# Projections of three attentions: biases added as PSUM is read, tables awaited apart, V taken by VectorE

## What is computed

```python
qkv = jnp.einsum('bsi,oi->bso', x, w_qkv) + b_qkv      # layer 0, self
q = _rope(q, cos, sin); k = _rope(k, cos, sin)         # r_even = even*cos - odd*sin; r_odd = even*sin + odd*cos
qh = _split_heads(q @ wq_w.T + wq_b)                   # layer 0, cross; kh, vh alike on ctx
return (x @ W.T + b).reshape(B, S, H, hd)              # layer 1, self: Q, K and V
```

## Time and profile before

| | |
|---|---|
| median of 3 runs | 9370.65 us |
| the profiled execution, its own time | 9320.69 us |
| its span | 9318.9 us |
| `l0ap_`: SyncE's first load to the last V copy | 28.2 to 206.1 us |
| `l0xp_`: the same | 934.7 to 1042.3 us |
| `l1ap_`: the same | 4400.5 to 4516.4 us |
| mean granted TensorE clock | 0.758 |

### The profile page before, as it was taken

How to read it: one execution, slowest core, us unless ns; L and a number is a source line. 1 busy time by engine, 2 the same in 40 slices (tenths; PEclk the granted TensorE clock), 3 DMA queues, 4 the chain that set the end, 5 groups by cost and what they waited for, 6 DMA issues and landing times. The chain is left out here.

```text
span 9318.9 us, 164285 instructions
## 1 busy us (share of the span) xinstructions
PE 6964.9 (75%) x31345; PEld 2804.8 (30%) x31468; DVE 6784.5 (73%) x47597; ACT 4490.9 (48%) x8515; POOL 3923.4 (42%) x2595
## 2 busy tenths in 40 slices
PE   6998667666666656999666666666656899999983
PEld 2333222222222224555222222222223322222212
DVE  2764599999999993554699999999997344344423
ACT  1564466666666652111476776677655322222220
POOL 0000255454545541221365656556553055555550
PEclk7998666666666665999666776766767999999986
DMA  2000000000000000000000000000000411111113
GB/s 62 26 21 5 34 5 8 5 8 5 8 6 7 8 1 16 14 20 10 35 5 8 5 8 5 8 5 8 5 5 9 161 30 29 29 40 32 29 30 73
DMA packets 81598, 193.31 MB, mean 21 GB/s; under 512 B 23728, under 2 KB 38062, under 8 KB 77230
## 3 DMA queue, kind: packets, MB, share of 16 engines
q1 hardware_dynamic: 72366, 169.98, 6.5%
q10 hardware_dynamic: 8192, 12.59, 0.5%
HBM read 118.97 MB, written 62.76 MB: 20 GB/s over the span
## 5 line engine op out<-in xcount | busy, mean ns | idle before, releaser
L2057 DVE TENSOR_REDUCE l1xc_part_max<-l1xc_by_query 128x1 f32<-128x512 f32 (+1 forms) x1024 | 558.0, 571 | 865.3 <-PE l1xc_by_query L1916 772.7
L557 PE MATMUL l1ac_by_query<-l1ac_k_stack,l1ac_q_stack 97*128 (+1 forms) x1024 | 441.5, 497 | 790.8 <-ACT keep_xT L652 436.3
L2015 ACT ACTIVATE l1xc_prob<-l1xc_less_max 128x512 f32<-128x512 f32 (+1 forms) x832 | 451.3, 594 | 1118.7 <-PE l1xc_less_max L1930 973.7
L745 DVE MAX8 l1ac_cand<-l1ac_score 128x8 f32<-128x32 f32 x8192 | 956.3, 185 | 27.9 <-ACT l1ac_score L652 16.9
L745 DVE MAX8 l1ac_cand<-keep_xT 128x8 f32<-128x32 f32 x8192 | 953.4, 183 | 4.4
L557 PE MATMUL l0xc_by_query<-l0xc_k_stack,l0xc_q_stack 97*128 (+2 forms) x1024 | 387.9, 448 | 724.2 <-ACT keep_xT L652 505.4
L745 DVE MAX8 l0xc_cand<-l0xc_score 128x8 f32<-128x25 f32 (+1 forms) x8192 | 896.0, 177 | 33.6 <-ACT l0xc_score L652 15.8
L745 DVE MAX8 l0xc_cand<-keep_xT 128x8 f32<-128x25 f32 (+1 forms) x8192 | 897.4, 177 | 4.4
L527 POOL TENSOR_SCALAR l1ac_lost<-l1ac_score,l1ac_tops 128x2048 bf16<-128x2048 f32 x128 | 695.8, 5436 | 472.8 <-DVE l1ac_tops L764 472.8
L1878 POOL TENSOR_TENSOR l1xc_total<-l1xc_total,l1xc_prob 128x2048 f32<-128x2048 f32 (+1 forms) x176 | 793.8, 4510 | 71.5 <-POOL l1xc_v_tile L1888 71.2
L527 POOL TENSOR_SCALAR l1ac_lost<-keep_xT,l1ac_tops 128x2048 bf16<-128x2048 f32 x128 | 696.1, 5438 | 271.6 <-DVE l1ac_tops L764 271.6
(11 more groups left out here) (455 smaller groups left out, 14631.2 us busy)
## 6 DMA issues: line engine op xcount, KB each, us to landing
l1xc_k<-wide_k SPq DMA_DIRECT2D x32, 400.2 KB, 5.2
moe_w<-in_L_ffn_mlp_w_dram SPq DMA_DIRECT2D x16, 512.0 KB, 4.2
wide_q<-l1xp_full SPq DMA_DIRECT2D x8, 1024.0 KB, 3.9
wide_q_parts<-l1xp_parts SPq DMA_DIRECT2D x16, 512.0 KB, 5.3
l1xc_q_hm<-wide_q_parts SPq DMA_DIRECT2D x32, 256.0 KB, 3.8
l1xc_q<-wide_q SPq DMA_DIRECT2D x32, 256.0 KB, 5.7
wide_sums<-l1xc_o_out ACTq DMA_DIRECT2D x64, 128.0 KB, 2.3
l1xf_num<-wide_sums SPq DMA_DIRECT2D x16, 512.0 KB, 11.7
```

The lines of the kernel that those rows point to most:

```text
L557: nc.tensor.matmul(sA[c % 2][:, 0:w], Qm[0:SHIFT_ROW, bass.ds(at + i * P, P)], Kb[0:SHIFT_ROW, bass.ds(at + a, w)], start=True, stop=True) ...
L745: seg = nc.vector.max(new[:, j:8 * NSEG:NSEG], score[i % 4][:, a:a + w])
L2015: nc.scalar.activation(prob[0:n, buf(j), c], yP[c % 2][0:n], ACT.Exp).then_inc(y_taken, 1)
L2057: nc.vector.tensor_reduce(part_max[:, i % 2, c:c + 1], a_bank(i, c)[:, 0:w], AX.X, ALU.max).then_inc(a_taken, 1)
```

## The change

Four things change in `project`.

1. No bias product is left in the loops of Q, K and V. A bias as a column (one value for each output feature) is made once: products of 128 columns by a single one (new L228) turn each row of 128 bias values into a column of the new PSUM bank `cols_bank`, and ScalarE copies them into `bias_cols`. With rotation VectorE adds the column and multiplies by the table in one instruction (new L316, L319), and the factor 0.25 of Q moves into the copies of the weights. Without it ScalarE adds the column in the copy out of PSUM (new L285, `Identity` with a bias operand where there was `Copy`).
2. The bias of V, which lies along the columns of a tile, is spread over 128 rows once by a product (new L221) into `v_bias`, and added as V is read.
3. Weights and biases have a semaphore of their own; TensorE waits for these six loads only. VectorE waits for the tables, and the mask has a third semaphore.
4. VectorE, not ScalarE, takes the tiles of V (new L303): two between the two subtractions of the last unit, the others behind the second. The mask row comes after them.

```diff
-            pe.wait_ge(loaded, n_loads * 16)
+            pe.wait_ge(loaded, 6 * 16)
...
+            nc.tensor.matmul(vbanks[0][:, 0:D], G.ones[0:1, 0:P], bias[:, 2, :], start=True, stop=True)
+            if rope:
+                pe.wait_ge(w_ready, 2 * W_STEPS)
+            for r in range(per):
+                for w in range(2):
+                    for oc in range(KC):
+                        row = (bias, biasR)[r] if rope else bias
+                        mm = nc.tensor.matmul(cols_bank[:, (r * 2 + w) * KC + oc:(r * 2 + w) * KC + oc + 1],
+                                              row[:, w, oc * P:(oc + 1) * P], G.ones[0:1, 0:1], start=True, stop=True)
+            mm.then_inc(cols_formed, 1)
...
-                    mm = nc.tensor.matmul(bank[:, 0:m], bt[:, w, oc * P:(oc + 1) * P], G.ones[0:1, 0:m],
-                                          start=False, stop=True)
                 mm.then_inc(formed, 1)
+            pe.wait_ge(cols_taken, 3)
             for t, (a, m) in enumerate(kt):
...
-                nc.tensor.matmul(vbanks[t % 2][0:m, 0:D], G.ones[0:1, 0:m], bias[:, 2, :],
-                                 start=False, stop=True).then_inc(v_formed, 1)
...
+            act.wait_ge(cols_formed, 1)
+            for w in range(2):
+                at = cols_bank[:, 0:4 * KC].rearrange("p (r w c) -> p r w c", r=2, w=2)
+                nc.scalar.activation(bias_cols[:, 0:per, w], at[:, 0:per, w], ACT.Copy, scale=SCALE[w]).then_inc(cols_taken, 1)
+            act.wait_ge(cols_taken, 2)
+            nc.scalar.activation(v_bias[:], vbanks[0][:, 0:D], ACT.Copy).then_inc(cols_taken, 1)
...
-                        nc.scalar.activation(full[:, u % 2, a:a + m], banks[at % 4][:, 0:m], ACT.Copy,
-                                             scale=0.25 if w == 0 else 1.0).then_inc(taken, 1)
+                        nc.scalar.activation(full[:, u % 2, a:a + m], banks[at % 4][:, 0:m], ACT.Identity,
+                                             scale=SCALE[w], bias=bias_cols[:, 0, w, oc:oc + 1]).then_inc(taken, 1)
...
-            for t, (a, m) in enumerate(kt):
-                act.wait_ge(v_formed, t + 1)
-                nc.scalar.activation(V[0:m, t].rearrange("p (h d) -> p h d", h=H),
-                                     vbanks[t % 2][0:m, 0:D].rearrange("p (h d) -> p h d", h=H),
-                                     ACT.Copy).then_inc(v_taken, 1)
...
+            def take_v(t):
+                m = kt[t][1]
+                dve.wait_ge(v_formed, t + 1)
+                nc.vector.tensor_tensor(V[0:m, t], vbanks[t % 2][0:m, 0:D], v_bias[0:m], ALU.add).then_inc(v_taken, 1)
+
             if rope:
-                dve.wait_ge(loaded, n_loads * 16)
+                dve.wait_ge(r_loaded, 2 * (P // DH) * 16)
+                dve.wait_ge(cols_taken, 2)
...
-                                                       scalar=scale, in1=cos[:, a:a + m], op0=ALU.mult,
-                                                       op1=ALU.mult).then_inc(r_chain, 1)
+                                                       scalar=bias_cols[:, 0, w, oc:oc + 1], in1=cos[:, a:a + m],
+                                                       op0=ALU.add, op1=ALU.mult).then_inc(r_chain, 1)
...
+                if u == len(units) - 1:
+                    dve.wait_ge(cols_taken, 3)
+                    for t in range(2):
+                        take_v(t)
                 dve.wait_ge(split, 3 * u + 2)
                 nc.vector.tensor_tensor(rest[:, 0:n], rest[:, 0:n], parts[:, u % 2, 1, 0:n],
                                         ALU.subtract).then_inc(rest_done, 1)
+            for t in range(2, len(kt)):
+                take_v(t)
```

More of the change, by code:

```diff
@@ L162, in project @@
         vbanks = [s.ps(f"vbank{b}", [P, CH]) for b in range(2)]
[L163 to L167, removed]
+        cols_bank = s.ps("cols_bank", [P, CH])
+        loaded, r_loaded, m_loaded, turned, w_ready = (s.sem(x) for x in (
+            "loaded", "r_loaded", "m_loaded", "turned", "w_ready"))
+        formed, taken, v_formed, v_taken, split, rest_done, masked, v_clear, cols_formed, cols_taken = (
+            s.sem(x) for x in ("formed", "taken", "v_formed", "v_taken", "split", "rest_done", "masked", "v_clear",
+                               "cols_formed", "cols_taken"))
+        stored = [s.sem("stored0"), s.sem("stored1")]
         roped, r_chain = s.sem("roped"), s.sem("r_chain")
-        n_loads = 6 + (16 if rope else 0) + (1 if mask is not None else 0)
         units = [(w, oc) for w in range(2) for oc in range(KC)]
@@ L224, in _ @@
                     bank = banks[(n * per + r) % 4]
-                    wt, bt = (wT, bias) if r == 0 else (wR, biasR)
+                    wt = wT if r == 0 else wR
                     for ic in range(KC):
-                        nc.tensor.matmul(bank[:, 0:m], wt[:, w, ic, oc * P:(oc + 1) * P],
-                                         src[w][:, ic, a:a + m], start=(ic == 0), stop=False)
-                    mm = nc.tensor.matmul(bank[:, 0:m], bt[:, w, oc * P:(oc + 1) * P], G.ones[0:1, 0:m],
-                                          start=False, stop=True)
+                        mm = nc.tensor.matmul(bank[:, 0:m], wt[:, w, ic, oc * P:(oc + 1) * P],
+                                              src[w][:, ic, a:a + m], start=(ic == 0), stop=(ic == KC - 1))
                 mm.then_inc(formed, 1)
+            pe.wait_ge(cols_taken, 3)
             for t, (a, m) in enumerate(kt):
@@ L245, in _ @@
                 bank = banks[i % 2][:].rearrange("p (c d) -> p c d", c=KC)
-                nc.scalar.activation(wT[:, i], bank, ACT.Copy).then_inc(w_ready, 1)
+                by = SCALE[i] if rope and i < 2 else 1.0
+                nc.scalar.activation(wT[:, i], bank, ACT.Copy, scale=by).then_inc(w_ready, 1)
                 if rope and i < 2:
@@ L249, in _ @@
                     out = wR[:, i].rearrange("p c (f two) -> p c f two", two=2)
[L250 to L251 removed]
+                    nc.scalar.activation(out[:, :, :, 0], pair[:, :, :, 1], ACT.Copy, scale=-by).then_inc(w_ready, 1)
+                    nc.scalar.activation(out[:, :, :, 1], pair[:, :, :, 0], ACT.Copy, scale=by).then_inc(w_ready, 1)
                     if i == 0:
[L253 removed]
+                        act.wait_ge(loaded, 6 * 16)
                     bp = bias[:, i].rearrange("p (f two) -> p f two", two=2)
@@ L290, in _ @@
                 if rope:
-                    scale = 0.25 if w == 0 else 1.0
                     for c, (a, m) in enumerate(chunks[u]):
```

27 lines of the change are left out of this document (14 added, 13 removed).

## The result

The changed kernel takes **9300.08 us** in the median of 4 runs (9293.61 to 9305.46), the one before beside it 9362.85 (9352.21 to 9376.61, 4 runs). The ratio is 0.9942, its 95% interval 0.9917 to 0.9967. It is faster, by 63 us where 125 were forecast, and 9300 lies 12 us above the upper end of the range. The profiled executions differ by still less: 9302.66 with a span of 9300.8, against 9320.69 with 9318.9. Their mean clocks are 0.756 and 0.758.

The account below looks back on a forecast made before the run. TensorE was taken to bound rotated units and V loops, ScalarE the units without rotation. Terms summed to -124.7 us: 9196 against the profiled 9320.69, 9246 against the 9370.65 median; range 9212 to 9288, chance 0.70.

Parts of the forecast that it names:

- head of layer 0: First projection's start: TensorE no longer waits for the sine table, first unit's last rotation ends at 58.8, not 79.1: -20.3 us.
- rotated units 2 to 4: First projection's later units: 22.0 us each against 23.8, including a 2.8 us clock restart in each: -5.4 us.
- V, layer 0: First projection's V loop: VectorE takes tiles, no bias products, tiles every 0.93 us at full clock: -32.0 us.
- cross, first unit: Cross-attention projection, first unit, bound by TensorE: 10.9 us instead of 16.9, -6.0 us.
- cross, other units: Cross-attention projection: fourth unit falls from 13.75 to ScalarE's own 10.1 us, -3.6; copies slowed by a pointer operand, +1.1.
- cross, V: Cross-attention projection's V loop, nine tiles after the last unit's splits: 20.0 us instead of 43.75, -23.8 us.
- layer 1, first unit: Layer 1 self-attention projection, first unit, bound by TensorE: ends at 4419.9 against 4423.7, -3.8 us.
- layer 1, other units: Layer 1 projection's units at ScalarE's pace: one pointer operand adds 0.09 us a copy, +1.1 us a stage.
- layer 1, V: Layer 1 projection's V loop, same 16 tiles as the first projection's: -32.0 us.
- T + 23.4: First projection's forecast V end, 23.4 us after T, the start of the last unit's first split; before, 55.4 us.
- Rival 1: V loops stay at half clock, tiles 1.9 us instead of 0.93: saving 97 us, time 9273; chance 0.15.
- Rival 3: Slower kernel: layer 1's unedited wide cross-attention falls to a lower mean clock, 123 us more at 0.86; chance 0.03.

## Why the prediction was right in the three stages and wrong on the time

By its own steps, from the first instruction of each stage:

| term | forecast | measured |
|---|---|---|
| head of layer 0 | -20.3 | -18.2 |
| rotated units 2 to 4 | -5.4 | -7.7 |
| V, layer 0 | -32.0 | -33.4 |
| cross, first unit | -6.0 | -5.2 |
| cross, other units | -3.6, +1.1 | -2.7 |
| cross, V | -23.8 | -24.8 |
| layer 1, first unit | -3.8 | -2.1 |
| layer 1, other units | +1.1 | +1.0 |
| layer 1, V | -32.0 | -34.3 |
| sum | -124.7 | -127.4 |

*Head.* Turning began at 34.48 (forecast 33.5) and the first rotation at 48.48 (forecast near 47). The 16 passes of one column took 42.6 - 39.27 = 3.3 us, not 1.0. The prediction had VectorE start when the sine table is there; the row at 48.48 names the first chunk (L241) as what came last.

*Rotated units.* They take 21.3 us, forecast 22.0. That TensorE would wait in each and start again at half clock is so, as two windows show, the wait and the burst after it:

```profile
86.50:91.60 5.10, 0.00 (x0) 0.00 (x0) 3.61 (x3) 2.74 (x2) 0.00 (x0) 0.95 0.00 0
91.60:94.00 2.40, 2.34 (x3) 1.17 (x4) 2.10 (x4) 0.63 (x1) 0.00 (x0) 0.50 0.40 157
```

The restart costs 3.58 - 1.88 = 1.7 us (a pair's row at full clock lasts 1.88), not the 2.8 of the earlier trace rows but the 1.7 of the earlier trace rows. That is 1.1 less than in the sum, where the unit came out 0.7 shorter: 19.2 + 1.7 = 20.9 against 21.3. "TensorE: Matmul & The Clock Gate" of the Trainium skill, section "HAM oscillation — how this bites in real kernels", says that bursts between waits restart slowly; this trace agrees, with 3.58 for the pair after a wait of 5.29.

*V.* The end was set at T + 23.4 and came at T + 22.0. A tile costs 0.86 us at full clock, not the 0.93 of the sum, which read a row's duration and not the distance of two starts. The clock did come back within the first two of the twelve tiles (0.56 from 133.6 to 135.7, 1.00 from 135.7 to 137); over the whole loop:

```profile
133.00:146.00 13.00, 11.66 (x49) 9.64 (x48) 6.40 (x16) 1.91 (x1) 0.00 (x0) 0.91 0.31 121
```

Rival 1 (V at half clock) is out, and the run with bias products kept shows why its evidence misled: those rows belong to a loop in which every third product has one row. This was the prediction's own argument against the rival.

*Pointers.* +0.09 forecast for the copy with one, 0.686 against 0.597 measured. On VectorE the same operand costs 0.06 (0.751 against 0.692 in L316), inside the chunk's time.

**The step that failed** reads: "The attention behind a projection starts only after a barrier, so whatever ends last in the stage counts in full, and nothing outside the three stages is touched." The first half holds. The second doesn't: the projections hand on results with other last bits, and the top-64 attentions branch on these. So the sum put at nothing a term that measured +78: three searches where there was one before, at 39 us each. Scaling Q by a factor of 1 + 1.5e-5 moves the number in either direction. The MAX8 over 128x2048 stood in the trace of before, x8 in a stage of 256 groups of 128 rows (L602 stands there x512, two passes a group), which told that it runs under a condition.

Rival 3 looked for an unedited stage that gets slower, but in the wide cross-attention and by its clock; that stage took 1672.2 us, 8.4 more than before, at the same clock of 0.93. In small it may be there: five profiles with the new projections have this stage at 1668.5 to 1689.0 us (clock 0.92 to 0.93), five with the old at 1659.3 to 1666.0 (0.93 to 0.94). No experiment took this up, and the sum had nothing for it.

With the searches counted the forecast for the profiled pair would have been 9320.69 - 124.7 + 78 = 9274. Measured is 9302.66: 25.8 of the 28.7 left is l1af's clock. Between the medians 127 - 78 = 49 us of saving are expected and 63 were measured; the other 14 lie within what the clock of the output rows moves from run to run. Whether the change moves the mean of these draws isn't shown. In l0xf and l1af short and long ones occur on either side (l1af at 55.3 and 81.4 with the old projections, at 55.4 and 81.1 with the new). In l0af they don't: 58.3, 58.3, 58.4, 80.1 and 80.3 with the old, 80.1 to 80.3 in all four profiles with the new projections and the old output rows. Four profiles are too few to call that an effect of the change.

A second weak step is the +-10 us for "the runs of before spread by 21 us". Three stages that each take 55 or 80 us can move a run by 75; later runs of the kernel before lay between 9297.55 and 9384.89. The lower bound is also off by its own sum, 9225 - 10 = 9215 and not 9212. A wider range would have held the 9300, with the searches still missing from the sum.

## What to carry to other kernels

Before forecasting a change of arithmetic, look for a register loaded from data and a branch on it, count in the trace how often it was taken and what it costs, and carry that as a term with both signs. A bias as a one-row product can be paid by the full products beside it too, as in the loop of V; look at the granted clock of the loop, and where it is at half with TensorE busy, take the product out first and move the take second. Where it is full, as in the loop of Q and K, only the product's own time is to be had. Where total times spread by more than the effect, compare stage by stage, and take the data-dependent work out of both sides.

## What the runs showed of the hardware

- The loop of V, in which one product in three has one row, stayed at half clock with TensorE busy 25.00 of 25 us (clock 0.50); without those products it ran at 0.88 to 0.91, restart included, with a tile every 0.86 us and not 3.15. The loop of Q and K, with the same share and products of 512 columns, ran at 1.00 (39.89 of 40 us busy). The three stages of output rows took 44 to 46 us without one-row products, in one profile, and 55 to 81 with them.
- With such products the same code of the output rows comes out at 55 to 60, 68 to 72 or 80 to 81 us, as the clock rises at the start, on the way or never; what decides it stays open.
- A search over the whole row costs VectorE 39 us in layer 1 and 31 in the cross-attention, and the attention doesn't hide it: the stages grow by 39.2 and 31.3.
- Sixteen passes of one column in a row took 3.3 us, 0.2 each, at a clock of 0.50, where the passes of one column in the earlier trace rows took 0.164.
